# Small steps of an attention moved to other slots, one transpose for four heads' maxima, and fills, a wait and a copy moved in the expert tiles

## The reference

```python
q = x.reshape(B, T, H, d) * scale          # x here: layernorm of x
k = cond_k.reshape(B, S, H, d) * scale     # cond_k and cond_v: ctx
scores = jnp.einsum('bthd,bshd->bhts', q, k)
w = jax.nn.softmax(scores.astype(jnp.float32), axis=-1)
out = jnp.einsum('bhts,bshd->bthd', w, v).reshape(B, T, W)
x = x + out @ w_proj.T + b_proj
x_n = layernorm(x)
top_v, top_i = jax.lax.top_k(x_n @ Wg.T, 2)   # gating: softmax over the two
hidden = jax.nn.silu(x_n @ W1[e].T) * (x_n @ W2[e].T)
return x + sum_e gating[e] * (hidden @ W3[e].T)
```

## Time and profile before

| | us |
|---|---|
| median of 3 runs | 885.71 (885.52 to 887.39) |
| the profiled execution | 885.23 |
| its span in the profile | 883.4 |

### The profile page before, as it was taken

The page is one execution under the profiler, slowest core; times in us unless marked ns, Lnnn a source line. Parts: engine busy times, 40 slices in busy tenths (PEclk is TensorE's granted clock), DMA queues, the critical chain, the costliest instruction groups (busy, mean ns, idle before and its releaser), DMA issues.

```text
span 883.4 us, 20060 instructions
## 1 busy us (share of the span) xinstructions
PE 789.3 (89%) x6472; PEld 481.7 (55%) x6472; DVE 602.3 (68%) x1224; ACT 557.1 (63%) x970; POOL 438.9 (50%) x431
## 2 busy tenths in 40 slices
PE   0578898989989898987989999997999999999995
PEld 0112233323333333332337788886888888888884
DVE  4898888979889798899815466553555555555552
ACT  3369789788898888867784544443444444444442
POOL 4565435786767778775634574223322222222222
PEclk9999999999999999999999999998999999999998
DMA  8585656866567585674285799998996788483822
GB/s 174 170 201 167 200 128 228 181 221 153 177 234 168 203 220 178 152 173 159 87 267 175 204 267 284 287 290 223 261 254 156 174 239 256 56 251 55 246 42 24
DMA packets 105955, 167.52 MB, mean 190 GB/s; under 512 B 54688, under 2 KB 83232, under 8 KB 101280
## 3 DMA queue, kind: packets, MB, share of 16 engines
q1 hardware_dynamic: 92448, 148.76, 58.4%
q0 software_dynamic: 13440, 17.90, 10.7%
HBM read 119.75 MB, written 42.55 MB: 184 GB/s over the span
## 4 chain that ended last, share of the span: by engine, by line
PE 45%; DMA 2%; ACT 2%; issue 2%; SPq 1%; POOL 1%; DVE 0%; POOLq 0%; ACTq 0%; DVEq 0%
PE ps L1371 9%; PE ps L1375 9%; PE ps L1373 9%; PE ps L1389 4%; PE ps L1393 4%; PE ps L1391 4%; PE ps L1294 2%; DMA slots<-fill 1%; ACT probs L839 1%; PE ps L1279 1%; POOL slots L472 1%; PE ps L1398 1%; DMA w<-w_parts 1%; SPq L534 1%; ACT z_n L844 1%
## 5 line engine op out<-in xcount | busy, mean ns | idle before, releaser
L970 DVE TENSOR_REDUCE neg_max<-ps 128x2 f16<-128x1024 f32 x256 | 309.1, 1221 | 38.1 <-PE ps L1266 33.6
L839 ACT ACTIVATE probs<-ps 128x1024 f32<-128x1024 f32 x256 | 258.9, 1024 | 62.1 <-PE ps L1279 61.6
L766 POOL DMA_INDIRECT out<-y,aim x72 | 113.1, 1570 | 246.8 <-DVE y L1197 174.1
L1371 PE MATMUL ps<-zt,w 128*128 128x256 f16 x792 | 217.2, 274 | 6.9 <-DMA w<-w_parts 5.2
L1375 PE MATMUL ps<-zt,w 128*128 128x256 f16 x792 | 217.1, 274 | 0.0
L1373 PE MATMUL ps<-zt,w 128*128 128x256 f16 x792 | 217.1, 274 | 0.0
L873 ACT ACTIVATE silu<-ps 128x256 f32<-128x256 f32 x216 | 82.5, 382 | 190.6 <-PE ps L1375 188.3
L1178 DVE SCALAR_TENSOR_TENSOR hid<-ps,silu 128x256 f32<-128x256 f32 x216 | 91.6, 425 | 133.9 <-ACT silu L873 130.5
L1294 PE MATMUL ps<-probs,v_ext 128*32 128x512 f32 x1024 | 139.8, 618 | 5.3 <-ACT heads L907 4.4
L1266 PE MATMUL ps<-k_stack,q_stack 48*128 48x512 f16 x512 | 104.4, 407 | 34.5 <-ACT probs L839 17.7
L1279 PE MATMUL ps<-q_stack,k_stack 49*128 49x512 f16 x512 | 102.3, 397 | 7.2 <-DVE neg_max L970 7.0
(11 more groups left out here) (126 smaller groups left out, 907.5 us busy)
## 6 DMA issues: line engine op xcount, KB each, us to landing
w<-w_parts SPq DMA_DIRECT2D x36, 1408.0 KB
w<-w_parts SPq DMA_DIRECT2D x36, 768.0 KB
w_in<-in_w SPq DMA_DIRECT2D x16, 704.0 KB, 5.2
v_ext<-in_v SPq DMA_DIRECT2D x8, 1024.0 KB, 5.5
k_stack<-k SPq DMA_DIRECT2D x48, 128.0 KB, 5.0
q_stack<-qt SPq DMA_DIRECT2D x48, 128.0 KB, 4.6
w_in<-in_w SPq DMA_DIRECT2D x8, 768.0 KB, 5.1
w_parts<-w_hi SPq DMA_DIRECT2D x16, 352.0 KB, 2.3
```

Source lines behind the costliest of these rows:

```text
L766: nc.gpsimd.indirect_dma_start(out=out, out_offset=bass.IndirectOffsetOnAxis(ap=aim[frm][:, t, 0:1].bitcast(U32), axis=0), in_=y[frm][:, t ...
L839: nc.scalar.activation(probs[g % 2][:, j:j + 2, k, :], pair_banks[PLACE["exp", u] % 3], ACT.Exp, scale=0.25).then_inc(s_exp, 1)
L970: nc.vector.tensor_reduce(neg_max[b % 2][:, i, c:c + 3:2], pair_banks[PLACE["max", u] % 3], AX.X, ALU.max, negate=True).then_inc(s_red, 1)
L1371: nc.tensor.matmul(dst, w[:, kk, 1, cols], z16[:, kk, :], start=(kk == 0), stop=False)
```

## The change

- **Maxima:** `neg_max` is laid out so that the four heads of a group and their four token blocks lie together, one transpose turns them into 16 rows of 128, ACT copies 16x128, and each of the two DMAs moves eight rows of 128 (256 bytes) where it moved two of 512 (1024 bytes).
- **Slots:** the table `HALF_MISC` and the numbers `AT_...` and `STEP_...` have other values. Maxima: 10, 16, 24, 33 become 8, 20, 24, 35. Projections 66 and 69 become 65 and 71; heads 0, turn 0, the second q turn, turns of z, logits and their turn move by one to four half-slots. The four z norms stand 3 + 1 in two slots instead of 4 in one.
- **Fills:** behind tiles 7 to 10 instead of 8 to 11. The first up-weight load of tile 12 is issued ahead of the waits for fills and scatters; tiles 12 and 13 are written out on SP.
- **Aim:** DVE's wait for scatter-adds of an earlier tile and the copy of `aim` stand behind the six hid steps instead of ahead of them.

The core of the diff:

```diff
-AT_CHOOSE = 44
+AT_CHOOSE = 45
-AT_K_IN = -22
-AT_K_LO = -4
-AT_K_PARTS = -6
-AT_MAX_ROW = 2
-AT_PICK = 49
+AT_K_IN = -32
+AT_K_LO = -7
+AT_K_PARTS = -16
+AT_MAX_ROW = -1
+AT_PICK = 50
-AT_Q_LO = -11
-AT_Q_PARTS = -4
-AT_SCATTER = 50
-AT_V_IN = 5
+AT_Q_LO = -9
+AT_Q_PARTS = -12
+AT_SCATTER = 53
+AT_V_IN = -7
-AT_W_LO = (3, 7, 14)
-AT_W_OUT = (1, 9, 13)
+AT_W_LO = (5, 9, 11)
+AT_W_OUT = (-4, 0, 7)
-AT_Z_LO = 40
-AT_Z_NORM = (37, 37, 37, 37)
-AT_Z_ROOT = 36
+AT_Z_LO = 45
+AT_Z_NORM = (37, 37, 37, 38)
+AT_Z_ROOT = 38
...
-                                         max_row[g % 2][2 * par:2 * par + 2, :]).then_inc(s_mrow[g], 16)
+                                         max_row[g % 2][2 * NT * par:2 * NT * (par + 1), :]).then_inc(s_mrow[g], 16)
...
-                for e in range((k - EARLY - 2) * 2, (k - EARLY - 1) * 2):
+                for e in range((k - EARLY - 1) * 2, (k - EARLY) * 2):
...
-            known_tiles(EARLY, EARLY + 2, load_rows, load_up, load_down)
+            known_tiles(EARLY, EARLY + 1, load_rows, load_up, load_down)
             sp.wait_ge(s_tab, K_EARLY_TAB + 1)
-            known_tiles(EARLY + 2, KNOWN, load_rows, load_up, load_down, pad_regions)
+            known_tiles(EARLY + 1, KNOWN - 1, load_rows, load_up, load_down, pad_regions)
+            known_tiles(KNOWN - 1, KNOWN, load_rows, load_up, load_down)
             total = tiles_in_use(sp)
+            known_tiles(KNOWN, KNOWN + 1, load_up)
             sp.wait_ge(f_pad, 16 * E)
...
-            firm_tiles(sp, KNOWN, FIRM_TILES, (load_rows, 0), (load_up, 0), (load_down, 0))
+            known_tiles(KNOWN, KNOWN + 1, load_rows, load_down)
+            known_tiles(KNOWN + 1, KNOWN + 2, load_rows, load_up, load_down)
+            firm_tiles(sp, KNOWN + 2, FIRM_TILES, (load_rows, 0), (load_up, 0), (load_down, 0))
...
-                        nc.scalar.copy(max_row[i % 2][:, :], misc16[0:4, 0:T]).then_inc(s_mr, 1)
+                        nc.scalar.copy(max_row[i % 2][:, :], misc16[0:4 * NT, 0:P]).then_inc(s_mr, 1)
...
-                nc.vector.tensor_copy(aim[to][:, :, :].bitcast(I32),
-                                      aim_in[par][:, :, :].bitcast(I32)).then_inc(f_aim, 1)
                 for m in range(HC + 1):
...
+                    if m == HC:
+                        if least >= KNOWN:
+                            dve.wait_ge(f_add, (k - 1) * 32)
...
+                        nc.vector.tensor_copy(aim[to][:, :, :].bitcast(I32),
+                                              aim_in[par][:, :, :].bitcast(I32)).then_inc(f_aim, 1)
...
-                        for t in range(NT):
-                            mm = nc.tensor.transpose(misc16[0:4, t * P:(t + 1) * P],
-                                                     neg_max[b % 2][:, t, 4 * i:4 * i + 4], ident16[:, :])
+                        by_head = neg_max[b % 2][:, i, :, :].rearrange("p h t -> p (h t)")
+                        mm = nc.tensor.transpose(misc16[0:4 * NT, 0:P], by_head, ident16[:, :])
```

More of the change, by code:

```diff
@@ L36 @@
 EARLY_BATCHES = 5
-assert EARLY % 2 == 0 and KNOWN % 2 == 0 and EARLY <= KNOWN <= 2 * T * EARLY_BATCHES // SLOTS - (E - 1)
+assert EARLY % 2 == 0 and KNOWN == EARLY + 2 + E // 2 and KNOWN <= 2 * T * EARLY_BATCHES // SLOTS - (E - 1)
 LATER = FFN_TILES - KNOWN
@@ L96 @@
 PER = H
-AT_CHOOSE = 44
-AT_CLEAR = -13
+AT_CHOOSE = 45
+AT_CLEAR = -15
 AT_EXP = 8
 AT_K_HI = -18
-AT_K_IN = -22
-AT_K_LO = -4
-AT_K_PARTS = -6
-AT_MAX_ROW = 2
-AT_PICK = 49
+AT_K_IN = -32
[3 more added lines that the diff above has]
+AT_PICK = 50
 AT_Q_HI = -13
-AT_Q_LO = -11
-AT_Q_PARTS = -4
-AT_SCATTER = 50
-AT_V_IN = 5
+AT_Q_LO = -9
+AT_Q_PARTS = -12
+AT_SCATTER = 53
+AT_V_IN = -7
 AT_WEIGH = 12
-AT_W_LO = (3, 7, 14)
-AT_W_OUT = (1, 9, 13)
[L114 to L118, removed]
-AT_Z_HI = 40
-AT_Z_LO = 40
-AT_Z_NORM = (37, 37, 37, 37)
-AT_Z_ROOT = 36
-STEP_LN2 = (124, 138, 145, 146, 147)
-STEP_PREP = (-98, -96, -94, -92, -79)
+AT_W_LO = (5, 9, 11)
+AT_W_OUT = (-4, 0, 7)
+AT_X2_OUT = 38
+AT_X_IN = -33
+AT_X_NORM = (-14, -16, -15, -14)
+AT_X_RES = 19
+AT_X_ROOT = -11
+AT_Z_HI = 40
+AT_Z_LO = 45
+AT_Z_NORM = (37, 37, 37, 38)
+AT_Z_ROOT = 38
+STEP_LN2 = (126, 136, 142, 145, 145)
+STEP_PREP = (-99, -96, -95, -91, -74)
 STEP_SLOT = 191
-STEP_TOP = 173
-STEP_TOP_INDEX = 173
-HALF_MISC = sorted([(-23, 'turn_q', 0), (-20, 'turn_q', 1), (10, 'max', 0), (16, 'max', 1), (24, 'max', 2), (33, 'max', 3), (39, 'heads', 0), (43, 'heads', 1), (49, 'heads', 2), (55, 'turn', 0), (57, 'heads', 3), (59, 'turn', 1), (61, 'project', 0), (63, 'project', 1), (66, 'project', 2), (69, 'project', 3), (77, 'turn_z', 1), (79, 'turn_z', 0), (83, 'logits', 0), (85, 'turn_l', 0), (94, 'prefix', 0)])
+STEP_TOP = 174
+STEP_TOP_INDEX = 177
+HALF_MISC = sorted([(-23, 'turn_q', 0), (-19, 'turn_q', 1), (8, 'max', 0), (20, 'max', 1), (24, 'max', 2), (35, 'max', 3), (37, 'heads', 0), (43, 'heads', 1), (49, 'heads', 2), (51, 'turn', 0), (57, 'heads', 3), (59, 'turn', 1), (61, 'project', 0), (63, 'project', 1), (65, 'project', 2), (71, 'project', 3), (78, 'turn_z', 0), (79, 'turn_z', 1), (85, 'logits', 0), (86, 'turn_l', 0), (94, 'prefix', 0)])
 FIRST, LAST = -27, PER * (B - 1) + 51
@@ L312, in build @@
         shift = sa("shift", [P, NT])
-        neg_max = [sa(f"neg_max{i}", [P, NT, H], F16) for i in range(2)]
-        max_row = [sa(f"max_row{i}", [4, T], F16) for i in range(2)]
+        neg_max = [sa(f"neg_max{i}", [P, 4, 4, NT], F16) for i in range(2)]
+        max_row = [sa(f"max_row{i}", [4 * NT, P], F16) for i in range(2)]
         recip = sa("recip", [P, NT, 4])
@@ L1180, in tile @@
                             in1=silu[m % 2][rows, :], op0=ALU.mult, op1=ALU.mult).then_inc(f_hid, 1)
+                    if m == HC:
+                        if least >= KNOWN:
+                            dve.wait_ge(f_add, (k - 1) * 32)
+                        elif least >= EARLY:
+                            dve.wait_ge(f_add, (k - EARLY + 1) * 32)
+                        dve.wait_ge(f_tok[par], half * 16 + 16)
+                        nc.vector.tensor_copy(aim[to][:, :, :].bitcast(I32),
+                                              aim_in[par][:, :, :].bitcast(I32)).then_inc(f_aim, 1)
                     if m >= 1:
```

11 lines of the change are left out of this document (3 added, 8 removed).

## The result

The changed kernel takes 880.57 us (median of 20 runs, 874.23 to 884.99) where the kernel before takes 883.97 (20 runs, 881.27 to 890.88): the ratio is 0.995, 95% interval 0.9931 to 0.9969. It is faster, by 0.5% (3.4 us between the medians); 12.3 us were forecast. The time lies inside the range and near rival 1 (879.5), whose reason holds only in part.

A forecast was written before the change was run, and what follows sets the result against it. PE, by far the busiest engine, was taken to bound the kernel through its standstills and slower clock. From 885.23 us, tile 12 -5.3, POOL's order -0.9 and attention -6.1 gave -12.3, so 873 us; range 865 to 882.

The forecast's parts named there:

- rival 1: POOL's loop takes the gain of batches 3 to 7 and tile 12's half-rate stretch stays: 879.5 us, chance 0.20.
- The beat: PE's M-score starts in the attention: 1.55 us an even half-slot, 1.28 an odd one, 2.83 a slot, 45.3 for 16.
- the excess per batch: Attention: a batch of 52.2 us has 6.9 us over its 16 slots, caused by the small operations.
- the hole and its shadow: Ahead of tile 12 PE waits 5.2 us for weights; behind it 5 us run at half clock, costing 2.5 us.
- what these gains meet: Batches 3 to 7: PE's gain meets POOL's chain, 0.2 us to spare; 0.4 booked each for 3 to 6, 0.5 for 7.
- The wait for the root: Batches 3 to 7: ACT's 0.22 us wait for z's root only lengthens, to near 1 us; PE's gain before it uncounted.
- Maxima: One transpose for four takes 0.37 us off each even half-slot turn; 24 turns, 8.9 us if all count; ends 0.19 and 0.5.
- Tile 12: Expert tiles: hole -3.9 us, half-rate stretch -2.5, DVE's later wait for scatter-adds +1.1; together -5.3 us.
- POOL's order: Tiles 0 to 6: a scatter-add moved from ahead of the norm's root halves PE's 1.84 us z_n wait; 0.9 saved.
- rival 2: SP's crowded queue makes w_in, split 2, choice and second rows of maxima late: slower, 888 us, chance 0.12.
- the attention: All batches: 2.2 us gained in 0 and 1, 1.8 in 2, 2.1 in 3 to 7; sum 6.1, between 2.5 and 11.
- Short transfers: Stacked rows of maxima in 256 B pieces: no loss taken; far end 0.6 us in each of 8 batches, 4.8 us.

The follow-up runs named there:

- z_late: Changed kernel with the z norms one slot later and their turns in half-slots 16 and 18 of the next batch; 878.38 us, ratio 0.9921 to the kernel before.
- mix2: Changed kernel with z norms, their turns and the second q turn later, nothing left out; 875.61 us, ratio 0.9892 to the kernel before.
- root_cut: Changed kernel with split 0's low half left out but for 128 columns, all experts but the first (weights wrong there); 864.97 us, ratio 0.9769 to the kernel before.
- aim_back: Changed kernel with DVE's wait for scatter-adds and the copy of aim ahead of the hid steps again; 889.2 us, ratio 1.0081 to the kernel before.
- tail_only: Kernel before with only the expert-tile edits (fills, tile 12's up load, DVE's wait and aim copy); 884.51 us, ratio 0.9986 to the kernel before.
- mix3: mix2 with Z_LO ahead of split 2 on POOL and the key loads behind w_in on SP; 900.97 us, ratio 1.017 to the kernel before.
- max_only: Kernel before with only the maxima's new layout, one transpose, copy and DMAs, in the old slots; 881.11 us, ratio 0.9948 to the kernel before.
- mix6: mix2 with only the rows of maxima one slot sooner on SP, ahead of the load of x; 874.66 us, ratio 0.9874 to the kernel before.

## Why the prediction was wrong, point by point

- **The bounds of PE were read rightly.** The beat, the excess per batch, the hole and its shadow were there, and the hole went. The direction was right.
- **The step that failed is "what these gains meet": POOL's loop was sized too short.** The working had the choice at 50.0 us after the pick and 0.8 from the prefix to the next pick, a loop of 50.8 that lets the gain pass. The loops measure 52.6 to 55.2, and the steady batches, booked at 1.6 us gained, lost 4.3. Three terms were wrong. Behind sel POOL has 1.5 us of its own, where 0.8 was taken from a kernel in which that work was done earlier. From the issue of w_in to its use pass 6.0 to 7.5 us, not 5.5. And in batches 3 and 5 the issue itself comes at 35.0 and 35.2, not 32: the key issues wait for the batch before's last scores, which the working left out.
- **The wait for the root was found, but its price was put at nothing.** The fixed time was right to 0.1 us (21.0 after the pick, measured 21.1), and the working said that what PE gains ahead of it "only lengthens that wait". In batch 4 that is nearly so: with the pause gone in `z_late` and `mix2` that batch wins 0.2 us at most. In batches 3 and 5 it costs more, for ACT's wait holds the exponentials, pauses of 0.97 and 0.50 on PE become one of 3 us, and the stretches at half clock double. They make the last scores and so the keys, w_in and sel late; without the pause sel of these batches is ready 2.5 to 3.4 us sooner (`z_late`, `mix2`). `root_cut` alone doesn't show this, since it shortens the whole loop.
- **Maxima**: 0.37 a turn was read off the even half-slot alone; the measured gain is about 0.2, and lies in the pair of halves. Batches 1 and 2 won 1.8 each, where 1.1 and 1.8 were summed; batch 0, where 1.1 was booked, was 0.9 longer.
- **Tile 12**: -5.3 was forecast and the profile shows -7.1, since DVE's wait is 0 and not 1.1, and of the hole nothing stays. But the working took the three edits as separate, and they are not: the fills with the aim copy in its old place cost more than they bring (`aim_back`, 365.9 us from tile 4 on against 364.4 before), both together on the old tables next to nothing (`tail_only`), and their full worth comes only with the scatter-adds ahead of the last scatters.
- **POOL's order** was priced at the wrong row. The z_n wait of 1.84 is 1.89 after, and a stretch at half clock from 504 to 508 follows it, +2.2 us. Its worth is at tile 12, where it takes away a backlog of adds.
- **Rivals, and luck.** Rival 1 had the size right, for half its reason: the loop took the gain, but the shadow of the hole did go. Of rival 2 the first half came about: w_in, split 2 and the choice were late, with periods like its 53.7, though half of the time by a late issue and not by the landing alone. Its second half, the rows of maxima, cost 3.0 us; `mix3` is where it decides. That the time still fell into the range is partly luck: the attention missed its sum by 6.3 us the wrong way, and the last part won 1.8 more than booked.
- **Short transfers.** The rule on transfers under 512 B (the Trainium skill, "DMA: Bandwidth & Descriptors", section Specifications) cost nothing that `max_only` shows: with the old slots PE never waited for those rows. The exception of its section "Why small descriptors are slow (HBM only)" agrees with that.

What stays open: why the changed kernel's own runs spread over 11 us (granted clock from 0.973 to 0.987 in the same runs, and the longest run has the lowest clock), and which of the early adds makes the late order so dear.

## What to carry to other kernels

Where one engine gets faster and meets another's loop, add up that loop to its end, from one turn to the same place in the next, with every wait inside it; here 0.7 us behind its last result, 0.5 to 2 in a load and 3 in the issue of that load were missing. Where it meets a fixed time, look at what is queued in order behind the wait, and whether the pause brings a slower stretch. Moving the waiting steps behind their fixed times won some 5 us more here (`mix2`, and surely `mix6`). And edits that uncover a wait and edits that take that wait away should be priced together, never one by one.

## What the runs showed of the hardware

- Pauses of PE of 3.25 and 2.97 us came with windows of 8 and 4 us at a mean granted clock of 0.57 in batches 3 and 5 of the changed kernel, but with none in batch 4 (granted clock 1.00), with the same pause of 2.97 us. So the pause alone doesn't decide it, and no run here told what does.
- A DMA of 4 kB inside the chip's own memory took 6.7 us from its issue to its first use behind 1.5 MB of loads issued in the 5.5 us before (`mix3`, batch 4). In `max_only`, where the second group's rows are issued ahead of those loads, PE never waited for them.
